# Local attention: probabilities divided before their transposition, attended rows straight out of PE in feature-major form

## The chip, the core and the metric

One core of one Trainium2 chip runs the whole program: a stack of four blocks over 8192 tokens of 128 features in float32. The metric is the device time of one execution in microseconds. The engines are PE (matrix products), DVE, ACT and POOL (elementwise work and reductions) and SP (transfers); each runs its own instruction list in order and waits on semaphores for the others. PE writes to eight banks (PSUM), 128 partitions x 512 float32 each, named `banks` in the rows; POOL cannot read them.

## The reference

The function touched is the local attention of the last block, in both of its layers (DEPTH = 2). The part that matters:

```python
q, k = l2norm(q) * q_scale, l2norm(k) * k_scale      # then rotary embedding
bk, bv = look_around(bk), look_around(bv)             # own window of 64 and the one before
sim = jnp.einsum('bhwid,bhwjd->bhwij', bq, bk)
sim = jnp.where(mask, -jnp.finfo(sim.dtype).max, sim)
attn = jax.nn.softmax(sim, axis=-1)
out = jnp.einsum('bhwij,bhwjd->bhwid', attn, bv)
# heads joined, out @ wo, added to the layer's input
```

Eight heads of 64 features, windows of 64 queries that see 128 keys. The softmax is exp(sim - row maximum) divided by the row's sum. Dividing commutes with the product with v, so it can be done before or behind it.

## The kernel before, in words

`local_attention` works in slots of one tile of 128 tokens; there are 64 slots in each layer, four in one round of a hardware loop (`rounds_of`). Slot k is software-pipelined over several tiles: it projects q and k of tile k+3, norms and rotates tile k+2, turns q and k of tile k+1, computes scores and exponentials of tile k, and multiplies tile k-1 with v. The order of work on each engine is what its own `slot(i, k)` writes down; nothing reorders it. Tiles with even k (L1852 in the scores) see the start of a sequence half, those with odd k (L1856) use `v_mixed`, which POOL puts together from two tiles' v.

One tile's path behind the scores, with names as in the rows:

- DVE reduces the raw scores (minus_raw, L2096) and scales the result (minus_max, L2100, from minus_raw and rnorm).
- ACT takes the exponentials of four heads (`exps(i, k, 0)`), later of the other four, with row sums (L2015). POOL's second cross product (L1925) also waits for minus_max.
- In the next slot PE transposes the probabilities of four heads (`pe_turn`, L1865), DVE copies them to SBUF (probs_t, L2080), PE multiplies with v (`pe_mix`, L1879) into bank 5, token-major; then the same for the other four heads.
- In the slot after that DVE takes the reciprocal of the row sums (L2085) and multiplies bank 5 by it (attended_tok, L2089); PE transposes the result in four pieces (L1995), ACT copies them to `ot` (L2060).
- One slot later still PE multiplies `ot` with the output weights (L1976) and DVE adds to xn (L2108).

Beside this DVE does the sums of squares (L2114), the straight part of the rotation (L2124, twice) and the sum with the crossed part (L2133, called the rotated sum below). POOL does the norm of k (L1935, `unit`), the crossed part of the rotation (L1925, twice), and, in turns, the shifted copy of tokens (L345, L346; even slots, once PE's v projection is through) or `v_mixed` (L1953, L1954; odd slots).

Banks 6 and 7 are shared in turn by the entries of MISC: the n-th use waits until the use two before it has been read.

## Time and profile before

| | us |
|---|---|
| median of 3 runs | 3130.24 (3124.16 to 3334.51) |
| profiled execution | 3113.36 |
| its span in the trace | 3111.6 |

| engine | busy us (share) | granted clock |
|---|---|---|
| PE | 2867.9 (92%) | 0.962 over the span |
| DVE | 2120.9 (68%) | |
| ACT | 2077.8 (67%) | |
| POOL | 1022.5 (33%) | |

The shares are means over all stages. Local attention is the stretch from about 1521 to 2140 us and that from about 2315 to 2940 us; between them and behind them stand the feed-forward parts. The ends of PE's instructions are modelled, and DVE's and POOL's instructions are recorded from the time they begin, held or not: an instruction that takes longer than its equals was held inside.

### The profile page before, as it was taken

The numbers are of one execution on the slowest core, as the hardware profiler recorded it, in microseconds if no ns is written. First come the engines' busy times: TensorE is split into PE (matmuls) and PEld (weight loads), VectorE is DVE, ScalarE is ACT, GpSimd is POOL, SyncE is SP. The second block draws the span as 40 slices with busy tenths as digits, with TensorE's granted clock in tenths as the row PEclk, the third lists the DMA queues.
The fourth block names the chain that finished last, engine by engine and source line by source line (L and its number), as shares of the span: only waits on it lengthen the run. The fifth ranks groups of instructions, "written<-read, shape, count | busy, mean of one in ns | idle before, by whom it ended". The sixth has DMA issues, their size and how long they took to land. (4 is left out here: it accounts for less than half of the span.)

```text
span 3111.6 us, 64366 instructions
## 1 busy us (share of the span) xinstructions
PE 2867.9 (92%) x19916; PEld 1800.0 (58%) x19916; DVE 2120.9 (68%) x3260; ACT 2077.8 (67%) x5545; POOL 1022.5 (33%) x1164
## 2 busy tenths in 40 slices
PE   6899999997999799778799999998989999999899
PEld 3577896763744234435466666665435666666543
DVE  4666555666844689657688878885437878888656
ACT  4466565667733744263388888886858888888686
POOL 0233343330000033110255555552225555555321
PEclk9899998999999999889899999998999999999999
DMA  4200220000000000220000000000000000000000
GB/s 137 75 20 21 59 66 18 20 17 12 1 15 1 0 1 1 55 31 0 26 2 0 0 0 0 0 0 19 1 8 2 0 0 0 0 0 0 1 21 34
DMA packets 82988, 51.48 MB, mean 17 GB/s; under 512 B 28848, under 2 KB 75568, under 8 KB 82864
## 3 DMA queue, kind: packets, MB, share of 16 engines
q1 hardware_dynamic: 78768, 41.56, 4.8%
q0 software_dynamic: 4096, 8.40, 0.9%
q8 instruction: 62, 1.02, 0.1%
q14 instruction: 62, 0.51, 0.1%
HBM read 31.59 MB, written 18.35 MB: 16 GB/s over the span
## 5 line engine op out<-in xcount | busy, mean ns | idle before, releaser
L1887 PE MATMUL banks<-weights,hf 128*128 128x512 f32 x768 | 436.8, 652 | 23.9 <-POOL hf L346 11.3
L2015 ACT ACTIVATE probs<-banks,minus_max,rnorm 128x128 f32<-128x128 f32 x1024 | 455.2, 465 | 3.1 <-DVE minus_max L2100 3.1
L1925 POOL TENSOR_TENSOR qk_cross<-qk_raw,rope_scaled 128x512 f32<-128x512 f32 x256 | 326.2, 1275 | 50.8 <-DVE minus_max L2100 33.3
L2080 DVE COPY probs_t<-banks 128x512 f32<-128x512 f32 x256 | 175.9, 687 | 134.6 <-PE banks L1865 134.0
L2015 ACT ACTIVATION_READ_ACCUMULATOR probs<-banks,minus_max,rnorm 128x1 f32 x1024 | 217.9, 213 | 0.0
L1935 POOL TENSOR_TENSOR qk_rot<-qk_rot,rnorm 128x512 f32<-128x512 f32 x128 | 133.6, 1044 | 256.4 <-DVE qk_rot L2133 244.0
L718 ACT ACTIVATE probs<-banks,minus_max 128x128 f32<-128x128 f32 (+1 forms) x512 | 208.3, 426 | 14.0 <-DVE minus_max L757 12.0
L2096 DVE TENSOR_REDUCE minus_raw<-banks 128x8 f32<-128x1024 f32 x128 | 156.8, 1225 | 55.5 <-PE banks L1852 32.4
L1879 PE MATMUL banks<-v_tok,probs_t 128*64 128x64 f32 x3072 | 174.6, 228 | 8.8 <-DVE probs_t L2080 3.8
L1879 PEld LDWEIGHTS banks<-v_tok,probs_t 128*64 128x64 f32 x3072 | 139.2, 137 | 71.4 <-issue 42.5
L2114 DVE TENSOR_REDUCE sumsq<-qk_sq 128x16 f32<-128x1024 f32 x128 | 154.8, 1209 | 27.0 <-issue 19.9
L2124 DVE TENSOR_TENSOR qk_rot<-qk_raw,rope_scaled 128x512 f32<-128x512 f32 x256 | 165.9, 689 | 5.8
L1896 PE MATMUL banks<-ident,qk_rot 128*128 128x128 f32 x1024 | 162.8, 282 | 4.7 <-DVE qk_rot L2133 4.7
L1887 PEld LDWEIGHTS banks<-weights,hf 128*128 128x128 f32 x768 | 117.2, 192 | 79.1 <-ACT kt L2041 21.2
L1865 PE MATMUL banks<-ident,probs 128*128 128x128 f32 x1024 | 160.8, 280 | 0.0
L2133 DVE TENSOR_TENSOR qk_rot<-qk_rot,qk_cross 128x1024 f32<-128x1024 f32 x128 | 159.2, 1244 | 0.2
L1865 PEld LDWEIGHTS banks<-ident,probs 128*128 128x128 f32 x1024 | 117.4, 141 | 71.9 <-issue 63.3
L756 DVE TENSOR_REDUCE minus_max<-banks 128x2 f32<-128x256 f32 x128 | 54.3, 424 | 124.8 <-PE banks L590 124.8
L1976 PE MATMUL banks<-ot,weights 128*128 128x128 f32 x1024 | 136.0, 276 | 1.6 <-ACT ot L2060 1.6
L345 POOL COPY hf<-xn 64x256 f32 (+1 forms) x64 | 57.8, 903 | 236.8 <-PE banks L1887 236.5
L2029 ACT ACTIVATE qk_sq<-qk_raw 128x1024 f32<-128x1024 f32 x128 | 134.3, 1049 | 0.1
L1896 PEld LDWEIGHTS banks<-ident,qk_rot 128*128 128x128 f32 x1024 | 114.9, 142 | 29.5 <-issue 21.0
(343 smaller groups left out, 7126.4 us busy)
## 6 DMA issues: line engine op xcount, KB each, us to landing
sorted_x<-zero_rows SPq DMA_DIRECT2D x10, 512.0 KB, 6.3
rows_in<-sorted_x SPq DMA_DIRECT2D x18, 256.0 KB, 3.1
sorted_y<-rows_out SPq DMA_DIRECT2D x18, 256.0 KB, 2.4
x_res<-in_x SPq DMA_DIRECT2D x8, 512.0 KB, 6.6
out_x<-x_res SPq DMA_DIRECT2D x16, 256.0 KB, 2.0
w1b<-in_L_ffn_w SPq DMA_DIRECT2D x8, 256.0 KB, 4.5
s_branch<-in_L_ffn_w SPq DMA_DIRECT2D x8, 256.0 KB, 6.5
w1g<-in_L_ffn_W SPq DMA_DIRECT2D x8, 256.0 KB, 3.0
```

The lines of the kernel that those rows point to most:

```text
L718: last = act.activation(pr[:, j % 2, e, span], ps[:, 2 * s + e, span], ACT.Exp, bias=nm[:, s, qb, e:e + 1], accum_out=sums[:, u, qb, head: ...
L1865: mm = pe.transpose(ps[:, 4, n * P:(n + 1) * P], pr[:, k % 2, 4 * h + n], m["ident"][:])
L1879: mm = pe.matmul(ps[64 * w:64 * w + 64, 5, at], pt[:, h, n * P + 64 * w:n * P + 64 * w + 64], vm[:, at] if tb and not w else va[:, k % 4, ...
L1887: pe.matmul(ps[:, misc(k, j)], hf[:, n // 2 % 2, 0, n % 2 * P:(n % 2 + 1) * P], wqkv[:, w:w + QW], start=True, stop=True).then_inc(*S[name ...
L1896: mm = pe.transpose(ps[:, misc(k, j), c * P:(c + 1) * P], st[:, n % 4, first:first + P], m["ident"][:])
L1925: return pool.tensor_tensor(by_half(tw[:, n, at]), by_half(qk[:, n, at])[:, :, ::-1, :], tab[:, n, 2 * w + 1].rearrange("p (a d) -> p a d" ...
L2015: last = act.activation(pr[:, k % 2, head], ps[:, 2 * (k % 2) + par, c * P:(c + 1) * P], ACT.Exp, scale=rn[:, k % 4, head:head + 1], bias= ...
L2080: dve.tensor_copy(pt[:, h], ps[:, 4]).then_inc(*S["turned_sb"].inc)
L2096: dve.tensor_reduce(nr[:].rearrange("p (b c) -> p b c", b=2), ps[:, 2 * (k % 2):2 * (k % 2) + 2].rearrange("p b (c t) -> p b c t", c=4), A ...
L2114: dve.tensor_reduce(ss[:], by_head(sq[:]), AX.X, ALU.add).then_inc(*S["sumsq"].inc)
L2124: last = dve.tensor_tensor(by_head(st[:, n, at]), by_head(qk[:, n % 2, at]), tab[:, n % 2, 2 * w:2 * w + 1].to_broadcast([P, HEADS, DH]), ...
L2133: dve.tensor_tensor(st[:, n], st[:, n], tw[:, n % 2], ALU.add).then_inc(*S["rotated"].inc)
```

## The change

The reciprocal and the division move in front of the transposition. For heads 4 to 7 DVE multiplies the probabilities of tile k-1 (`half`), for heads 0 to 3 POOL does (`weigh`), in one product of 128x512 each. `pe_mix` now takes v as the weights and probs_t as what streams, so that a head's rows come out of PE with the features on the partitions; ACT copies bank 5 to `ot`, and L1995, L2089 and bank uses of the transposed result go. The output projection and the addition to xn come one slot earlier, and at another place in the slot.

```diff
-MISC = [("qt_sb", 1), ("added", -3), ("q_sb", 3), ("kt_sb", 1), ("k_sb", 3), ("v_sb", 1), ("ot_sb", -2)]
+MISC = [("qt_sb", 1), ("q_sb", 3), ("kt_sb", 1), ("k_sb", 3), ("v_sb", 1), ("added", -2)]
...
         def pe_turn(pe, i, k, h):
-            pe.wait_ge(*S["exps"].at(i, 2 * k + h))
+            pe.wait_ge(*S["masked" if h else "weighed"].at(i, k))
...
+            width = P // (1 + tb)
             for n in range(4):
-                at = slice((4 * h + n) * DH, (4 * h + n + 1) * DH)
-                for w in range(2):
-                    mm = pe.matmul(ps[64 * w:64 * w + 64, 5, at], pt[:, h, n * P + 64 * w:n * P + 64 * w + 64],
-                                   vm[:, at] if tb and not w else va[:, k % 4, at], start=True, stop=True)
+                head = 4 * h + n
+                at = slice(head * DH, (head + 1) * DH)
+                rows = slice(head % 2 * 64, head % 2 * 64 + 64)
+                for w in range(1 + tb):
+                    first = head // 2 * P + w * width
+                    mm = pe.matmul(ps[rows, 5, first:first + width],
+                                   vm[:, at] if tb and not w else va[:, k % 4, at],
+                                   pt[:, h, n * P + w * width:n * P + (w + 1) * width], start=True, stop=True)
...
+                def weigh(i, k):
+                    pool.wait_ge(*S["rowsum"].at(i, 2 * k))
+                    pool.tensor_tensor(pr[:, k % 2, 0:4], pr[:, k % 2, 0:4],
+                                       rs[:, k % 2, 0:4].unsqueeze(2).to_broadcast([P, 4, P]), ALU.mult)\
+                        .then_inc(*S["weighed"].inc)
...
                         pool.wait_ge(*S["copied"].at(i, k // 2 + 2))
+                    if here(i, k):
+                        weigh(i, k)
...
                     if here(i, k - 2):
-                        pe_free(pe, i, k, OT_AT)
-                        pe.wait_ge(*S["attended"].at(i, k - 2))
+                        pe_free(pe, i, k, OUT_AT)
+                        pe.wait_ge(*S["ot_sb"].at(i, k - 2))
                         for c in range(4):
-                            mm = pe.transpose(ps[:, misc(k, OT_AT), c * P:(c + 1) * P], o[:, c * P:(c + 1) * P],
-                                              m["ident"][:])
-                        mm.then_inc(*S["ot_ps"].inc)
+                            mm = pe.matmul(ps[:, misc(k, OUT_AT), 0:P], wo[:, c], ot[:, c], start=(c == 0), stop=(c == 3))
+                        mm.then_inc(*S["o_ps"].inc)
...
                 def slot(i, k):
+                    if here(i, k - 2):
+                        act.wait_ge(*S["mixed"].at(i, 2 * (k - 2) + 1))
+                        act.wait_ge(*S["o_ps"].at(i, k - 3))
+                        act.activation(ot[:], bank(ps, 5, 4, P), ACT.Copy).then_inc(*S["ot_sb"].inc)
...
+                def inverse(i, k, h):
+                    heads = slice(4 * h, 4 * h + 4)
+                    dve.wait_ge(*S["exps"].at(i, 2 * k + h))
+                    if h == 0:
+                        dve.wait_ge(*S["weighed"].at(i, k - 2))
+                    dve.reciprocal(rs[:, k % 2, heads], sums[:, k % 2, heads]).then_inc(*S["rowsum"].inc)
...
+                    if here(i, k - 1):
+                        inverse(i, k - 1, 1)
+                        dve.wait_ge(*S["rowsum"].at(i, 2 * (k - 1) + 1))
+                        half = pr[:, (k - 1) % 2, 4:]
+                        dve.tensor_tensor(half, half, rs[:, (k - 1) % 2, 4:].unsqueeze(2).to_broadcast([P, 4, P]), ALU.mult)\
+                            .then_inc(*S["masked"].inc)
                     if here(i, k - 1):
                         turned(i, k - 1, 0)
```

On DVE, a slot in the middle of the loop, before and then now (L2080 and L2089 COPY are the same copies; line numbers moved by nine or more):

```order
L2096 TENSOR_REDUCE minus_raw<-banks 128x8 [waits rowmax,rnorm,scores]
L2100 TENSOR_TENSOR minus_max<-minus_raw,rnorm 128x8 [waits rawmax]
...
L2108 TENSOR_TENSOR xn<-xn,banks 128x128
...
L2080 COPY probs_t<-banks 128x512 [waits mixed]
...
L2080 COPY probs_t<-banks 128x512 [waits mixed,turned]
L2133 TENSOR_TENSOR qk_rot<-qk_rot,qk_cross 128x1024 [waits crossed,straight]
...
L2085 RECIPROCAL inv_sums<-row_sums 128x8 [waits exps]
...
L2089 TENSOR_TENSOR attended_tok<-banks,inv_sums 128x512 [waits ot_ps,mixed]
```

```order
L2103 TENSOR_REDUCE minus_raw<-banks 128x8 [waits rowmax,rnorm,scores]
L2107 TENSOR_TENSOR minus_max<-minus_raw,rnorm 128x8 [waits rawmax]
...
L2096 RECIPROCAL inv_sums<-row_sums 128x4 [waits exps]
...
L2115 TENSOR_TENSOR probs<-probs,inv_sums 128x512 [waits rowsum]
...
L2089 COPY probs_t<-banks 128x512 [waits mixed]
...
L2096 RECIPROCAL inv_sums<-row_sums 128x4 [waits weighed]
...
L2089 COPY probs_t<-banks 128x512 [waits mixed]
L2143 TENSOR_TENSOR qk_rot<-qk_rot,qk_cross 128x1024 [waits crossed,straight]
...
L2148 TENSOR_TENSOR xn<-xn,banks 128x128
```

A reciprocal and a product of the probabilities now stand between minus_max and the first turned copy, a second reciprocal in front of the second copy; the addition to xn went from the slot's front to its end.

On POOL, an even slot's end and the next slot's start in the loop now; before, the same rows without L1937:

```order
L1930 TENSOR_TENSOR qk_cross<-qk_raw,rope_scaled 128x512 [waits rowmax]
...
L345 COPY hf<-xn 64x256
...
L346 COPY hf<-xn 64x255
...
L1937 TENSOR_TENSOR probs<-probs,inv_sums 128x512 [waits rowsum]
L1946 TENSOR_TENSOR qk_rot<-qk_rot,rnorm 128x512 [waits rotated,rnorm]
...
L1930 TENSOR_TENSOR qk_cross<-qk_raw,rope_scaled 128x512 [waits rotated,k_sb,q_sb]
```

POOL's product stands last in its slot, in front of the norm of the next tile's k and its two cross products.

On PE, from the value projection to the q transposes of the next slot, before and now:

```order
L1887 MATMUL banks<-weights,hf 128x512
L1995 MATMUL banks<-ident,attended_tok 128x128 x4
...
L1879 MATMUL banks<-v_tok,probs_t 64x64 x8
L1845 MATMUL banks<-hide,ident_bf 128x512 x2
L1852 MATMUL banks<-kt,qt 128x128 x8
...
L1896 MATMUL banks<-ident,qk_rot 128x128 x4
...
L1976 MATMUL banks<-ot,weights 128x128 x4
```

```order
L1892 MATMUL banks<-weights,hf 128x512
L2006 MATMUL banks<-ot,weights 128x128 x4
...
L1883 MATMUL banks<-probs_t,v_tok 64x128 x4
...
L1845 MATMUL banks<-hide,ident_bf 128x512 x2
L1852 MATMUL banks<-kt,qt 128x128 x8
...
L1901 MATMUL banks<-ident,qk_rot 128x128 x4
...
L1892 MATMUL banks<-weights,hf 128x512
```

The output projection took the place of the four transposes, and the q projection follows the q transposes directly. In the rows of the trace every float32 product is two instructions (two passes), a transposition one.

## Rows read from the trace of the kernel before

**Rows 1.** Busy time of the engines in one stretch: us, busy (xinstructions), PEclk, DMA share, GB/s.
```profile
1700.00:1800.00 100.00, 99.19 (x993) 66.52 (x993) 81.15 (x129) 85.56 (x265) 55.29 (x55) 1.00 0.00 0
```
**Rows 2.** Row-maximum reduction in 1600 to 2050: xcount, ns min/median/max, first and last start.
```profile
L2096 DVE TENSOR_REDUCE minus_raw<-banks x48: 1223/1225/1226, 1600.5 to 2042.2; 128x8 f32<-128x1024 f32 x48
```
**Rows 3.** Instructions of DVE in order: start us, us, what, idle before.
```profile
1732.13 1.23 DVE L2096 TENSOR_REDUCE minus_raw<-banks 128x8 f32<-128x1024 f32 x1 [0.57 <-PE banks L1852]
1733.39 0.17 DVE L2100 TENSOR_TENSOR minus_max<-minus_raw,rnorm 128x8 f32<-128x8 f32 x1
1733.68 0.29 DVE L2108 TENSOR_TENSOR xn<-xn,banks 128x128 f32 x1
1735.02 0.69 DVE L2080 COPY probs_t<-banks 128x512 f32<-128x512 f32 x1 [1.05 <-PE banks L1865]
...
1738.33 0.68 DVE L2080 COPY probs_t<-banks 128x512 f32<-128x512 f32 x1
1738.93 1.21 DVE L2133 TENSOR_TENSOR qk_rot<-qk_rot,qk_cross 128x1024 f32<-128x1024 f32 x1
1740.07 0.19 DVE L2085 RECIPROCAL inv_sums<-row_sums 128x8 f32<-128x8 f32 x1
1740.45 0.69 DVE L2089 TENSOR_TENSOR attended_tok<-banks,inv_sums 128x512 f32<-128x512 f32 x1 [0.19 <-DVE inv_sums L2085]
1741.59 1.22 DVE L2096 TENSOR_REDUCE minus_raw<-banks 128x8 f32<-128x1024 f32 x1 [0.45 <-PE banks L1856]
...
1744.40 0.69 DVE L2080 COPY probs_t<-banks 128x512 f32<-128x512 f32 x1 [0.97 <-PE banks L1865]
```
**Rows 4.** Instructions of PE in the same stretch.
```profile
1737.62 1.12 PE L1887 MATMUL banks<-weights,hf 128*128 128x512 f32 x2
1738.58 0.60 PE L1995 MATMUL banks<-ident,attended_tok 128*128 128x128 f32 x4
1739.72 0.60 PE L1845 MATMUL banks<-hide,ident_bf 128*128 128x512 bf16 x2
...
1741.79 1.06 PE L1976 MATMUL banks<-ot,weights 128*128 128x128 f32 x8
1742.71 1.12 PE L1887 MATMUL banks<-weights,hf 128*128 128x512 f32 x2
```
**Rows 5.** Instructions of POOL in the same stretch.
```profile
1733.64 1.27 POOL L1925 TENSOR_TENSOR qk_cross<-qk_raw,rope_scaled 128x512 f32<-128x512 f32 x1 [0.68 <-DVE minus_max L2100]
1738.94 1.46 POOL L345 COPY hf<-xn 64x256 f32 x1 [4.03 <-PE banks L1887]
1740.44 0.40 POOL L346 COPY hf<-xn 64x255 f32 x1
1740.92 1.04 POOL L1935 TENSOR_TENSOR qk_rot<-qk_rot,rnorm 128x512 f32<-128x512 f32 x1
```
**Rows 6.** DVE and POOL meeting: two instructions in order, and three lines in 1600 to 2050.
```profile
1555.39 0.63 DVE L2100 TENSOR_TENSOR minus_max<-minus_raw,rnorm 128x8 f32<-128x8 f32 x1
...
1554.73 2.64 POOL L1925 TENSOR_TENSOR qk_cross<-qk_raw,rope_scaled 128x512 f32<-128x512 f32 x2
...
L2100 DVE TENSOR_TENSOR minus_max<-minus_raw,rnorm x48: 166/214/371, 1601.8 to 2043.5; 128x8 f32<-128x8 f32 x48
L1925 POOL TENSOR_TENSOR qk_cross<-qk_raw,rope_scaled x96: 1265/1274/1286, 1600.4 to 2043.9; 128x512 f32<-128x512 f32 x96
L345 POOL COPY hf<-xn x24: 391/924/1461, 1607.1 to 2039.6; 64x256 f32 x24
```
**Rows 7.** PE during the first mix of an odd tile, in order.
```profile
1736.35 0.27 PE L1879 MATMUL banks<-v_mixed,probs_t 128*64 128x64 f32 x1
...
1736.46 0.22 PE L1879 MATMUL banks<-v_mixed,probs_t 128*64 128x64 f32 x1
1736.46 0.22 PE L1879 MATMUL banks<-v_tok,probs_t 128*64 128x64 f32 x1
1736.52 0.22 PE L1879 MATMUL banks<-v_mixed,probs_t 128*64 128x64 f32 x1
...
1736.97 0.44 PE L1865 MATMUL banks<-ident,probs 128*128 128x128 f32 x2
```

More of the change, by code:

```diff
@@ L1780, in conv_mixer @@
         S["loaded"].base += 16 * len(ahead)
-MISC = [("qt_sb", 1), ("added", -3), ("q_sb", 3), ("kt_sb", 1), ("k_sb", 3), ("v_sb", 1), ("ot_sb", -2)]
-QT_AT, OUT_AT, Q_AT, KT_AT, K_AT, V_AT, OT_AT = range(7)
+MISC = [("qt_sb", 1), ("q_sb", 3), ("kt_sb", 1), ("k_sb", 3), ("v_sb", 1), ("added", -2)]
+QT_AT, Q_AT, KT_AT, K_AT, V_AT, OUT_AT = range(6)
 def local_weights(area, a, layer):
@@ L1813, in local_attention @@
         nr, nm = buf("minus_raw", P, HEADS), buf("minus_max", P, 2, HEADS)
-        sums, rs = buf("row_sums", P, 2, HEADS), buf("inv_sums", P, HEADS)
-        o, ot = buf("attended_tok", P, QW), buf("ot", P, 4, P)
+        sums, rs = buf("row_sums", P, 2, HEADS), buf("inv_sums", P, 2, HEADS)
+        ot = buf("ot", P, 4, P)
         def here(i, n, per=4):
@@ L1871, in pe_mix @@
             if h == 0:
-                pe.wait_ge(*S["attended"].at(i, k - 1))
+                pe.wait_ge(*S["ot_sb"].at(i, k - 1))
                 pe.wait_ge(*S["v_sb"].at(i, k))
@@ L1900, in local_attention @@
                              "rnorm", "crossed", "rotated", "unit", "qt_ps", "kt_ps", "qt_sb", "kt_sb", "scores",
-                             "rawmax", "rowmax", "rowsum", "attended", "ot_ps", "ot_sb", "o_ps", "added"], 4)
-        per.update(copied=2, v_mixed=2, g2=2, exps=8, turned=8, turned_sb=8, mixed=8)
+                             "rawmax", "rowmax", "ot_sb", "o_ps", "added"], 4)
+        per.update(copied=2, v_mixed=2, g2=2, exps=8, rowsum=8, weighed=4, masked=4, turned=8, turned_sb=8, mixed=8)
         with Stage(R, **per), nc.Block() as block:
@@ L1951, in slot @@
                             pool.wait_ge(*S["crossed"].at(i, k + 2))
+                        if here(i, k - 1):
+                            pool.wait_ge(*S["weighed"].at(i, k - 1))
                         pool.sem_inc(S["g2"].sem, 1)
@@ L1971, in slot @@
                         pe_turn_qk(pe, i, k, QT_AT, "qt")
-                    if here(i, k - 3):
-                        pe_free(pe, i, k, OUT_AT)
-                        pe.wait_ge(*S["ot_sb"].at(i, k - 3))
-                        for c in range(4):
-                            mm = pe.matmul(ps[:, misc(k, OUT_AT), 0:P], wo[:, c], ot[:, c], start=(c == 0), stop=(c == 3))
-                        mm.then_inc(*S["o_ps"].inc)
                     if here(i, k + 3):
@@ L2009, in exps @@
                     act.wait_ge(*S["turned"].at(i, 2 * (k - 2) + h))
[L2010 to L2011 removed]
+                    act.wait_ge(*S["rowsum"].at(i, 2 * (k - 2) + h))
                     for n in range(4):
@@ L2056, in slot @@
                         act.activation(va[:, (k + 1) % 4], ps[:, misc(k, V_AT)], ACT.Copy).then_inc(*S["v_sb"].inc)
-                    if here(i, k - 2):
-                        act.wait_ge(*S["ot_ps"].at(i, k - 2))
-                        act.wait_ge(*S["o_ps"].at(i, k - 3))
-                        act.activation(ot[:], bank(ps, misc(k, OT_AT), 4, P), ACT.Copy).then_inc(*S["ot_sb"].inc)
                     if here(i, k):
@@ L2103, in slot @@
                             .then_inc(*S["rowmax"].inc)
-                    if here(i, k - 3):
-                        xn = m["xn"][:, bass.ds((i * 4 + k - 3) * P, P)]
-                        dve.wait_ge(*S["o_ps"].at(i, k - 3))
-                        dve.wait_ge(S["first"].sem, PRIME)
-                        dve.tensor_tensor(xn, xn, ps[:, misc(k, OUT_AT), 0:P], ALU.add).then_inc(*S["added"].inc)
+                    if here(i, k - 1):
+                        inverse(i, k - 1, 1)
[3 more added lines that the diff above has]
+                            .then_inc(*S["masked"].inc)
                     if here(i, k - 1):
@@ L2126, in slot @@
                         last.then_inc(*S["straight"].inc)
+                    if here(i, k):
+                        inverse(i, k, 0)
                     if here(i, k - 1):
@@ L2133, in slot @@
                         dve.tensor_tensor(st[:, n], st[:, n], tw[:, n % 2], ALU.add).then_inc(*S["rotated"].inc)
+                    if here(i, k - 2):
+                        xn = m["xn"][:, bass.ds((i * 4 + k - 2) * P, P)]
+                        dve.wait_ge(*S["o_ps"].at(i, k - 2))
+                        dve.wait_ge(S["first"].sem, PRIME)
+                        dve.tensor_tensor(xn, xn, ps[:, misc(k, OUT_AT), 0:P], ALU.add).then_inc(*S["added"].inc)
                 rounds_of(dve, R, 1, 1, lambda i: [slot(i, k) for k in range(4)])
```

13 lines of the change are left out of this document (2 added, 11 removed).

## The prediction, made before the changed kernel was timed

> **What bounds the kernel now.** The diff touches one function, `local_attention`, which runs once for each of the two layers; so I first read busy time by stage, then the engines' rows over two neighbouring slots. In a stretch in the middle of the first layer [rows 1] the granted clock is 1.00 (the 2.4 GHz level) and PE is recorded as busy 99%, ACT 86%, DVE 81%, POOL 55%. PE's ends are modelled, so the 99% alone does not make PE the bound. The pace is the distance between two starts of the row-maximum reduction, one per slot: 48 of them from 1600.5 to 2042.2 us [rows 2], so 441.7 / 47 = 9.40 us. There are 64 slots in each of two layers, 128 x 9.40 = 1203 us of the 3113.4 us of the profiled execution.
>
> What paces a slot is read from DVE and PE together. Let R be the start of the reduction in the even slot, 1732.13 [rows 3]. The first turned copy (probs_t) starts at R+2.89, released by PE's transposes after an idle 1.05. The second turned copy starts at 1738.33, 3.31 later, with DVE busy all the way between them. PE's second mix needs that copy; the next mask matmul (L1845), which is queued right behind the mix, starts at 1739.72 [rows 4], 1.39 later; and the scores behind it let the next reduction start at 1741.59, 1.87 later. 2.89 + 3.31 + 3.26 = 9.46. So a slot is a loop: DVE work, mix, scores, DVE work. The only slack in it on DVE is the 0.97 to 1.05 in front of the first turned copy, and there PE is what is late: between scores and the transposes of the probabilities it does the q transposes, the output projection L1976 (0.92 to L1887, 1741.79 to 1742.71) and the q projection [rows 4].
>
> **The change, part by part.**
>
> *PE.* The four transposes L1995 go (0.60), and the output projection moves from its place in front of the q projection into theirs. They stood while PE was going to wait for the second turned copy anyway, so taking them out gives nothing by itself. Moving the projection brings the transposes of the probabilities 0.92 forward, to about R+1.9. In its new place it follows the value projection; behind the end of the first turned copy PE has a mix (0.62, 1736.35 to 1736.97 [rows 7]), transposes 0.60, value projection 0.96 (1737.62 to 1738.58 [rows 4]) and output projection 0.92 = 3.1 us, against 3.4 us that DVE takes from that end to the end of the second copy. Hidden, with 0.3 to spare.
>
> *The mixes.* In even slots eight 64x64 products become four of 64x128, alternating between the two column halves: the same time. In odd slots the two windows of one head now come one after the other in the same half. Before, neighbours in different halves start together, a pair every 0.06 us (1736.46, 1736.52 [rows 7]). If starts must keep the order of the program, the second window of a head waits 0.11 for the first (two passes), but the next head's first can run beside it, so a mix grows by one such step, 0.11. Bounds: 0, if the halves run freely, and 0.44 if nothing overlaps at all. I take 0.05 of the second mix in every odd slot, 62 x 0.05 = 3 us; the first mix has PE slack. The Trainium skill (TensorE: Matmul & The Clock Gate, Part 3, packing small matmuls) says that matmuls keep program order in start and end; by that the term would be 7 us, and without it 0.
>
> *ACT.* The copy to `ot` changes place and source, no work is added. The second half's exponentials start earlier by the length of that copy. ACT is idle in 14% of a slot, 1.3 us, and nothing in the loop above waits for it. Nothing.
>
> *DVE, without regard to POOL.* The product behind the mix goes (0.69, with its wait for the reciprocal 0.38 from start to start [rows 3]); it stood where DVE waited for scores, so this gives nothing. In the loop two things are added. Between the row maximum and the first turned copy: a reciprocal in the place of the addition to xn (R+1.55, as 1733.68), 0.38 later the product of four heads, R+1.93, and with 0.69 for it (the row of attended_tok, the same 128x512) and the usual start 0.08 before the predecessor's end, the first turned copy at R+2.54. That is 0.35 earlier than now. Between the two copies: a second reciprocal, 0.12 to 0.19, so 3.43 for 3.31. A slot would be 2.54 + 3.43 + 3.26 = 9.23.
>
> *POOL, and what it does to DVE.* POOL gets one more product (128x512, as L1935, 1.04 [rows 5]); with 55% of 9.4 busy, 5.2 us, it has the time. But the new DVE product reads two tensors in SBUF, and it comes just when POOL works. The second of POOL's two cross products waits for the row maximum: it starts at 1733.64 [rows 5], R+1.51, 0.08 after DVE's minus_max ends, and takes 1.27 [rows 6], to R+2.78. What happens when two such meet is in the trace. The tiny minus_max (128x8) takes 0.17 when POOL is idle and 0.63 at 1555.39, where it ends at 1556.02; POOL's first cross product ran from 1554.73 to 1556.00 [rows 6]. In the stretch its times run from 166 to 371 ns. The other way round, POOL's copy L345 takes 391 ns or 1461: the long one starts at 1738.94 beside DVE's rotated sum, which runs from 1738.93 to 1740.14, and ends 0.26 behind it [rows 3, 5]. So a DVE product of two SBUF tensors and a reading POOL instruction do not overlap: who is first finishes. DVE's addition to xn and its copies from the banks are not held. The Trainium skill (SBUF — State Buffer, SBUF: two separate sides) states this as an exclusive lock on a shared pair of ports, taken for the whole instruction by whoever starts first, for DVE instructions with two SBUF inputs against POOL instructions that read SBUF. By that rule the sum is slower than before, without it the 9.23 above holds; the trace agrees with it.
>
> The new product is ready at R+1.93, POOL began at R+1.51: it is held until POOL is through. minus_max ended 0.02 after POOL with 0.17 of its own, so it effectively began 0.15 before POOL's end; the product then ends at 2.78 - 0.15 + 0.69 = 3.32, and the turned copy starts at 3.24. Even slot: 3.24 + 3.43 + 3.26 = 9.93.
>
> In the odd slot POOL is later. At the end of the even one it has its two copies, the new product and `unit` (1.04) to do. The rotated sum starts at R+3.24+3.43+0.60 = 7.27 and ends at 8.48; POOL's product, queued behind the copies at about 7.4, is held to 8.4 and ends at 9.4; unit ends at 10.45, the first cross product at 11.77. The next reduction is at 9.93, so minus_max, held as before, ends at 1.86 instead of 1.43, and all behind it is 0.43 later: 10.36. Behind the odd slot (no shift copies, so POOL's product comes first, from 7.25 to 8.3, and holds the rotated sum to an end of 9.36, which is not in the loop) unit begins at 9.5 and the cross product ends at 11.8, 1.45 behind the next reduction: minus_max ends at 1.47 for 1.43, which I leave out. A pair of slots: 20.29 against 18.80, +1.49. I count 31 pairs per layer (the first and last slots are not in the steady order): 62 x 1.49 = +92 us.
>
> *The end of each layer.* Reciprocal, product and transposes (0.19 + 0.69 + 0.60) leave the drain: -3 us in two layers.
>
> **Sum:** 92 + 3 - 3 = +92 us on 3113.4, so 3205. The runs shown have a median of 3130.2, 17 us above the profiled execution; I take half of that and predict **3213 us**, 2.7% over the median. For one measurement 2%, 63 us, is about what can be told from no change.
>
> **The rivals.**
>
> 1. *The product comes first* (0.18). If reciprocal and product get in before POOL's cross product begins to read, POOL waits and DVE does not: 9.23 a slot, 124 x -0.17 = -21 us, some 3092 to 3109 us: not slower. For it: only 0.4 us lie between them. Against: POOL needs one semaphore after minus_max (0.08), DVE a whole reciprocal and its completion. It decides at 1.51 against 1.93. The same time comes out if the hold does not apply to a product with a repeated operand.
> 2. *POOL falls behind in every slot* (0.10). Then minus_max is held in even slots too, and shift copies that slip between two DVE products cost 0.4 in every other slot: 124 x 0.96 + 25 = +144, 3257 to 3274 us. It needs unit to begin later than 0.9 before the next reduction; even slots are past that by 0.4 and odd ones just on it, so a little more delay on POOL decides. Against: in odd slots POOL's product has no DVE product in front of it.
> 3. *Others* (0.08): PE's longer waits (0.4 to 1.3 us a slot) let the granted clock fall to its 1.2 GHz level in part of the stage, far slower (0.01); the holds hit but are half as long, within 2% (0.03); DVE's path is shorter than I think and more than 2% is gained, for which no row speaks (0.04).
>
> Forecast: 0.64, and of this 0.08 lies under 2% (if the odd slot is not delayed: 124 x 0.53 = 66, less the drain: 3176 to 3193). Slower: 0.56 + 0.10 + 0.01 = 0.67. Same: 0.08 + 0.18 + 0.03 = 0.29. Faster: 0.04. The range is 3100 to 3268: it takes in the forecast with both bounds, most of rival 2 and the upper part of rival 1. The forecast's own range is 3176 to 3240.
>
> **What would show it.** Right: the new DVE product of the probabilities recorded at about 1.4 us instead of 0.69, ending with POOL's second cross product; minus_max at about 0.6 in every other slot; reductions 10.1 us apart; PE idle more, its mix still released by the turned copy; ACT with 2 us of idle time. Wrong: the product at 0.7 and the cross product recorded as longer than 1.27 (rival 1); a pace under 9.4; the second mix released by the output projection instead of DVE; the new odd mix longer than 0.8 us.

## The result, and the profile after

The changed kernel takes 3202.8 us (median of 4 runs, 3201.7 to 3205.6) against 3131.2 us beside it: ratio 1.0239, 95% interval [1.0226, 1.0252]. It is slower by 2.4%. The forecast was 3213 us, the range 3100 to 3268, and "slower by over 2%" had 0.67. Ratios leave out two executions of the kernel before in a slow state of the chip, 3334.5 us and one of 7150.0 us beside e5 to e8.

The first view is the same stretch as in [rows 1], then the line of the row-maximum reduction as in [rows 2], with the lines that meet on DVE and POOL below it (count, ns min/median/max, first and last start).

```profile
1700.00:1800.00 100.00, 87.35 (x797) 56.66 (x798) 89.23 (x131) 79.86 (x250) 59.81 (x60) 1.00 0.00 0
```
```profile
L2103 DVE TENSOR_REDUCE minus_raw<-banks x45: 1223/1224/1226, 1602.1 to 2044.4; 128x8 f32<-128x1024 f32 x45
L2107 DVE TENSOR_TENSOR minus_max<-minus_raw,rnorm x45: 166/541/616, 1603.4 to 2045.7; 128x8 f32<-128x8 f32 x45
L2115 DVE TENSOR_TENSOR probs<-probs,inv_sums x45: 1733/1771/1779, 1604.1 to 2046.3; 128x512 f32<-128x512 f32 x45
L1937 POOL TENSOR_TENSOR probs<-probs,inv_sums x45: 1039/1799/1814, 1599.9 to 2042.1; 128x512 f32<-128x512 f32 x45
L1930 POOL TENSOR_TENSOR qk_cross<-qk_raw,rope_scaled x90: 1265/1271/1282, 1602.6 to 2046.3; 128x512 f32<-128x512 f32 x90
```

PE fell from 99% busy to 87%, DVE rose from 81% to 89%, at the same granted clock of 1.00 (2.4 GHz). The pace is 442.3 / 44 = 10.05 us a slot, against 9.40. Every one of the 45 products on DVE took 1.73 to 1.78 us, though its equal took 0.69 in [rows 3]; POOL's cross products kept their 1.27 [rows 6]. So where these two meet, DVE pays and POOL does not.

Two slots of DVE after (start, duration, what, idle before), to be laid beside [rows 3], and POOL beside [rows 5]:

```profile
1732.83 1.22 DVE L2103 TENSOR_REDUCE minus_raw<-banks 128x8 f32<-128x1024 f32 x1 [0.57 <-PE banks L1852]
1734.08 0.41 DVE L2107 TENSOR_TENSOR minus_max<-minus_raw,rnorm 128x8 f32<-128x8 f32 x1
1734.42 0.17 DVE L2096 RECIPROCAL inv_sums<-row_sums 128x4 f32<-128x4 f32 x1
1734.62 1.77 DVE L2115 TENSOR_TENSOR probs<-probs,inv_sums 128x512 f32<-128x512 f32 x1
1736.32 0.68 DVE L2089 COPY probs_t<-banks 128x512 f32<-128x512 f32 x1
...
1739.65 0.66 DVE L2089 COPY probs_t<-banks 128x512 f32<-128x512 f32 x1
1740.23 1.22 DVE L2143 TENSOR_TENSOR qk_rot<-qk_rot,qk_cross 128x1024 f32<-128x1024 f32 x1
...
1742.73 1.22 DVE L2103 TENSOR_REDUCE minus_raw<-banks 128x8 f32<-128x1024 f32 x1 [1.10 <-PE banks L1856]
1743.99 0.61 DVE L2107 TENSOR_TENSOR minus_max<-minus_raw,rnorm 128x8 f32<-128x8 f32 x1
```
```profile
1733.20 2.64 POOL L1930 TENSOR_TENSOR qk_cross<-qk_raw,rope_scaled 128x512 f32<-128x512 f32 x2
...
1740.53 1.81 POOL L1937 TENSOR_TENSOR probs<-probs,inv_sums 128x512 f32<-128x512 f32 x1 [0.16 <-POOL hf L346]
1742.30 1.04 POOL L1946 TENSOR_TENSOR qk_rot<-qk_rot,rnorm 128x512 f32<-128x512 f32 x1
1743.31 2.64 POOL L1930 TENSOR_TENSOR qk_cross<-qk_raw,rope_scaled 128x512 f32<-128x512 f32 x2
```

POOL's second cross product ends at 1733.20 + 2.64 = 1735.84, DVE's product at 1736.39: 0.55 apart, the product's own 0.69 less 0.14. The reverse case is at 1740.23: DVE's rotated sum runs to 1741.45 and POOL's product, 1.04 by itself, is recorded as 1.81.

DVE's copies, its sums of squares and its addition to xn are as short as before.

What PE waited for in 1600 to 2050 (us in total, times, longest), with 44 slots in the stretch. The same view of the kernel before has no line at all: PE waited for nobody.

```profile
PE banks L1883 <- DVE probs_t L2089: 37.8, 78, 0.8
PE banks L1892 <- ACT qk_raw L2048: 18.2, 45, 0.5
```

The whole span grew by 88.9 us (3111.6 to 3200.5). Within the layers, from the first to the last of 64 reductions, it is 43.0 + 44.1 = 87.1; another 8.1 lies ahead of the first reduction (1546.2, now 1554.3), and the stretch between the layers is 6.1 shorter. The 8.1 is not a cost of the loop: in the kernels of this study that first reduction falls anywhere from 1538.9 to 1563.9, although nothing ahead of the function differs. It goes with the group of runs and not with the edit: 1538.9 to 1544.9 in e1 to e4, 1559.6 to 1563.9 in e5 to e8, 1555.7 to 1559.6 in e9 and e10, and each group ran on a chip of its own. All that lies outside the two layers does the same: 1928.4 to 1929.6 us in e1 to e4, 1949.8 to 1952.9 in e5 to e8, 1944.0 and 1944.3 in e9 and e10, 1939.8 in the change, 1938.0 before. What differs between the groups is not known. For this reason the table below also gives the length of the two layers added up, which this scatter doesn't touch.

That column has a weakness of its own. It is one trace for each kernel, and the traced execution of the kernel before, 3113.4 us, is 17.8 us below the median of the runs beside the change, while that of the change lies on its median. By medians the change costs 71.7 us, by the traces 88.9. In which stage the other executions of the kernel before spend the 17 us is not shown. So the column carries comparisons between the changed kernels; against the kernel before, differences under some 18 us need the ratio as well.

| kernel | median us | ratio to before | slot us | two layers us |
|---|---|---|---|---|
| before | 3131.2 | 1 | 9.40 | 1173.6 |
| the change | 3202.8 | 1.0239 [1.0226, 1.0252] | 10.05 | 1260.7 |
| e1_fills | 3088.1 | 0.9922 [0.9891, 0.9953] | 9.23 | 1157.1 |
| e2_no_product | 3087.4 | 0.9920 [0.9888, 0.9951] | 9.24 | 1156.4 |
| e3_swap | 3128.0 | 1.0052 [1.0038, 1.0067] | 9.62 | 1201.1 |
| e4_cross_late | 3141.6 | 1.0090 [1.0064, 1.0117] | 9.69 | 1212.5 |
| e5_banks | 3127.3 | 0.9998 [0.9977, 1.0018] | 9.40 | 1175.3 |
| e6_moved | 3172.2 | 1.0132 [1.0111, 1.0154] | 9.77 | 1220.4 |
| e7_free | 3161.0 | 1.0102 [1.0083, 1.0122] | 9.64 | 1207.8 |
| e8_qfirst | 3215.9 | 1.0278 [1.0255, 1.0301] | 10.07 | 1261.0 |
| e9_late | 3119.7 | 0.9967 [0.9953, 0.9981] | 9.35 | 1170.8 |
| e10_late_mix | 3114.7 | 0.9949 [0.9933, 0.9966] | 9.32 | 1166.4 |

(e1 to e4 ran beside a median of 3111.1 us of the kernel before, e5 to e8 beside 3130.8, e9 and e10 beside 3130.7. e1 and e2 leave out a part of the work: e1 the crossed part of the rotation, e2 the division of heads 4 to 7.)

### The profile page after: what moved, and what is told of

Its sections match the earlier page's. It is cut to its first block and busy times, and to the rows that moved or that the text cites. A ratio compares the mean times of both kernels' runs of the same rounds, so it can differ in the third digit from the quotient of the medians.

```text
span 3200.5 us, 61524 instructions
## 1 busy us (share of the span) xinstructions
PE 2812.7 (88%) x18380; PEld 1737.6 (54%) x18380; DVE 2293.6 (72%) x3388; ACT 2077.6 (65%) x5545; POOL 1151.0 (36%) x1292
## 5 line engine op out<-in xcount | busy, mean ns | idle before, releaser
L1892 PE MATMUL banks<-weights,hf 128*128 128x512 f32 x768 | 417.7, 627 | 67.8 <-ACT qk_raw L2048 52.8
L1937 POOL TENSOR_TENSOR probs<-probs,inv_sums 128x512 f32<-128x512 f32 x128 | 177.8, 1389 | 176.3 <-DVE inv_sums L2096 166.6
L1883 PE MATMUL banks<-probs_t,v_tok 128*64 128x128 f32 (+1 forms) x2048 | 158.3, 255 | 73.8 <-DVE probs_t L2089 73.5
L2115 DVE TENSOR_TENSOR probs<-probs,inv_sums 128x512 f32<-128x512 f32 x128 | 219.1, 1712 | 4.4
L2143 DVE TENSOR_TENSOR qk_rot<-qk_rot,qk_cross 128x1024 f32<-128x1024 f32 x128 | 190.6, 1489 | 0.1
L1883 PEld LDWEIGHTS banks<-probs_t,v_tok 128*64 128x64 f32 x2048 | 113.6, 138 | 137.8 <-DVE probs_t L2089 137.1
L2089 DVE COPY probs_t<-banks 128x512 f32<-128x512 f32 x256 | 171.2, 669 | 6.4 <-PE banks L1865 6.3
L2037 ACT ACTIVATE qt<-banks 128x512 f32<-128x512 f32 x128 | 76.5, 598 | 150.5 <-PE banks L1901 150.5
L2006 PEld LDWEIGHTS banks<-ot,weights 128*128 128x128 f32 x1024 | 135.9, 194 | 61.1 <-issue 61.1
L1946 POOL TENSOR_TENSOR qk_rot<-qk_rot,rnorm 128x512 f32<-128x512 f32 x128 | 133.3, 1042 | 87.1 <-DVE qk_rot L2143 83.9
L2006 PE MATMUL banks<-ot,weights 128*128 128x128 f32 x1024 | 136.8, 277 | 1.6 <-ACT ot L2033 1.6
```

The lines of the kernel that those rows point to most:

```text
L1883: mm = pe.matmul(ps[rows, 5, first:first + width], vm[:, at] if tb and not w else va[:, k % 4, at], pt[:, h, n * P + w * width:n * P + (w ...
L1892: pe.matmul(ps[:, misc(k, j)], hf[:, n // 2 % 2, 0, n % 2 * P:(n % 2 + 1) * P], wqkv[:, w:w + QW], start=True, stop=True).then_inc(*S[name ...
L1937: pool.tensor_tensor(pr[:, k % 2, 0:4], pr[:, k % 2, 0:4], rs[:, k % 2, 0:4].unsqueeze(2).to_broadcast([P, 4, P]), ALU.mult)\
L2006: mm = pe.matmul(ps[:, misc(k, OUT_AT), 0:P], wo[:, c], ot[:, c], start=(c == 0), stop=(c == 3))
L2089: dve.tensor_copy(pt[:, h], ps[:, 4]).then_inc(*S["turned_sb"].inc)
L2115: dve.tensor_tensor(half, half, rs[:, (k - 1) % 2, 4:].unsqueeze(2).to_broadcast([P, 4, P]), ALU.mult)\
```

## The experiments

The theory: DVE's product and POOL's second cross product both read two tensors in SBUF and don't overlap, and DVE is second. The rivals: the product is slow by itself, or any work of POOL slows it, or the loss is PE's new order. First both sides of the meeting are taken away, then its timing is changed, then the operand.

**e1_fills: POOL writes instead of reading.**

```diff
-                        cross(i, k, 0)
+                        fill(i, k, 0)
...
+                def fill(i, k, w):
+                    pool.memset(tw[:, (k + 2) % 2, w * QW:(w + 1) * QW], 0.0)
+                    return pool.memset(spare[:, (k + 2) % 2, w, :], 0.0)
```

> POOL's two cross products of a slot are replaced by fills that write the same place and a spare buffer in about the same time (0.53 + 0.67 us each) but read nothing; the crossed part of the rotation is left out of the result. Theory (a DVE product of two SBUF tensors waits for a POOL instruction that reads SBUF): DVE's product of the probabilities falls from 1.77 to about 0.69 us and minus_max to 0.17, the pace from 10.05 to about 8.8 us a slot, the total to about 3045 us. Rival 1 (any work of POOL, also mere writing, slows DVE): product and pace stay, about 3200 us. Rival 2 (the product is slow by itself, from its in-place or repeated operand): product stays at 1.77, about 3200 us.

```profile
1738.77 0.17 DVE L2112 TENSOR_TENSOR minus_max<-minus_raw,rnorm 128x8 f32<-128x8 f32 x1
1738.86 0.18 DVE L2101 RECIPROCAL inv_sums<-row_sums 128x4 f32<-128x4 f32 x1
1739.08 0.69 DVE L2120 TENSOR_TENSOR probs<-probs,inv_sums 128x512 f32<-128x512 f32 x1
```
```profile
1738.84 0.64 POOL L1938 MEMSET spare<- 128x660 f32 x1
1739.43 0.52 POOL L1937 MEMSET qk_cross<- 128x512 f32 x1
1739.90 0.64 POOL L1938 MEMSET spare<- 128x660 f32 x1
```

DVE's product takes 0.69 while POOL is writing the whole time, and in all 49 slots of the stretch it takes 691 to 693 ns. So a busy POOL isn't enough: it must read. The whole loss is gone and more, 87.1 us turn into -16.5. The pace expected was 8.8 and came out 9.23. PE's waits say why: DVE never holds it up now, and it waits 19.8 us in 49 places, all for ACT's copy of the queries. The floor is PE's.

```profile
PE banks L1892 <- ACT qk_raw L2053: 19.8, 49, 0.5
```

**e2_no_product: the other side taken away.**

```diff
-                        dve.tensor_tensor(half, half, rs[:, (k - 1) % 2, 4:].unsqueeze(2).to_broadcast([P, 4, P]), ALU.mult)\
-                            .then_inc(*S["masked"].inc)
+                        dve.reciprocal(spare[:], sums[:, (k - 1) % 2, 4:]).then_inc(*S["masked"].inc)
```

> DVE's product of the probabilities is replaced by a second tiny reciprocal with the same semaphores; the division of heads 4 to 7 is left out. It prices the product in its place. Theory (product plus hold lie on the path): the pace falls by 1.3 to 1.6 us a slot until PE's own work of some 8.4 us is near, total 3005 to 3045 us. Rival (only the product's own 0.69 us counts, the hold falls into time that is waited anyway): about 3115 us. Rival (the loop is set by PE): under 20 us gained.

The layers have the same length as in e1 within 0.7 us, 1156.4. The pace fell by 0.81 us to 9.24, not by the expected 1.3 to 1.6, since PE's floor lies there and not at 8.4. POOL's products stand, minus_max is still held (166 to 772 ns), and it costs nothing, since DVE has time before PE needs it. So the product's 1.77 is what carries the loss. Whether its own 0.69 would matter this run can't tell; e1 has it and is as fast.

**e3_swap: the turned copy first.**

```diff
+                        turned(i, k - 1, 0)
+                    if here(i, k - 1):
                         inverse(i, k - 1, 1)
...
-                    if here(i, k - 1):
-                        turned(i, k - 1, 0)
```

> On DVE the first turned copy goes in front of the reciprocal and product of heads 4 to 7; nothing else changes. Theory (the loss is the place: the product arrives while POOL's second cross product reads): copy and mix no longer wait for it and it arrives 0.9 us later, so it is held 0.2 to 0.5 us instead of 1.1; about 9.3 us in even and 9.65 us in odd slots, total 3110 to 3145 us, about the kernel before. Rival (the product costs its queue time wherever it stands before the second copy): 3180 to 3205 us.

The product comes later and meets less of the cross product: 727/981/1179 ns for 1771. Of the 87.1 us 59.6 come back; the median, 3128.0, lies in the expected 3110 to 3145. What is left is the rest of the hold and minus_max, up to 961 ns, and PE still waits for probs_t, 12.4 us in 23 places. A reordering lessens such a hold and doesn't end it.

**e4_cross_late: POOL waits for DVE's product.**

```diff
                         cross(i, k, 0)
-                        if here(i, k):
-                            pool.wait_ge(*S["rowmax"].at(i, k))
+                        if here(i, k - 1):
+                            pool.wait_ge(*S["masked"].at(i, k - 1))
```

> POOL's second cross product waits for DVE's product of the probabilities instead of for minus_max. Theory: the product is held only by what is left of the first cross product, it takes 0.7 to 1.1 us instead of 1.77; the hold comes back in part at the rotation's straight products in odd slots (v_mixed copies later); 9.3 to 9.55 us a slot, total 3107 to 3139 us. Rival (POOL's whole chain sets the pace, so that a later cross product only delays it): 3200 us or more.

```profile
1742.80 0.93 DVE L2107 TENSOR_TENSOR minus_max<-minus_raw,rnorm 128x8 f32<-128x8 f32 x1
1743.65 0.17 DVE L2096 RECIPROCAL inv_sums<-row_sums 128x4 f32<-128x4 f32 x1
1743.85 0.69 DVE L2115 TENSOR_TENSOR probs<-probs,inv_sums 128x512 f32<-128x512 f32 x1
```
```profile
1742.43 1.27 POOL L1930 TENSOR_TENSOR qk_cross<-qk_raw,rope_scaled 128x512 f32<-128x512 f32 x1
1744.62 1.28 POOL L1930 TENSOR_TENSOR qk_cross<-qk_raw,rope_scaled 128x512 f32<-128x512 f32 x1 [0.92 <-DVE probs L2115]
```

The product is 0.69 in all 46 slots: the same instruction as in the change, the same operands, only not beside a reading POOL. That a product of two SBUF tensors with a repeated operand is slow by itself is excluded. The product is also still written in its own place, so that is excluded too. But the holds come back elsewhere: the other cross product now holds minus_max (to 1743.73; up to 980 ns in the stretch), the straight products of the rotation take up to 1096 ns for 688, and PE waits for probs_t 17.1 us in 23 places. The slot is 9.69, over the 9.3 to 9.55 that was expected. 48.2 of the 87.1 us come back.

**e5_banks: one operand from the banks.** ACT writes the exponentials of heads 4 to 7 back into their score banks; DVE's product reads them there.

```diff
-                        last = act.activation(pr[:, k % 2, head], ps[:, 2 * (k % 2) + par, c * P:(c + 1) * P], ACT.Exp,
+                        score = ps[:, 2 * (k % 2) + par, c * P:(c + 1) * P]
+                        last = act.activation(score if h else pr[:, k % 2, head], score, ACT.Exp,
...
-            pe.wait_ge(*S["exps"].at(i, 2 * (k - 2) + 1))
+            pe.wait_ge(*S["masked"].at(i, k - 2))
```

> ACT writes the exponentials of heads 4 to 7 back into the score banks, and DVE's product reads them there, so that it has one operand in SBUF (the reciprocals) instead of two; work, order and size are the same, POOL is as it was. Theory (only an instruction with two SBUF operands is held by a reading POOL): the product takes 0.69 us and is not held, minus_max still is (0.2 to 0.6); the pace is 9.3 to 9.45 us, or PE's floor of 9.22 where the other two kernels without the hold stood; ratio to the kernel before 0.990 to 1.003, about 3100 to 3140 us on the first chip. Rival (any DVE instruction beside POOL's products is slowed, or it is the repeated operand that is slow): product at 1.4 to 1.8 us, ratio about 1.024.

```profile
1746.64 0.17 DVE L2108 TENSOR_TENSOR minus_max<-minus_raw,rnorm 128x8 f32<-128x8 f32 x1
1746.75 0.18 DVE L2097 RECIPROCAL inv_sums<-row_sums 128x4 f32<-128x4 f32 x1
1746.96 0.69 DVE L2116 TENSOR_TENSOR probs<-banks,inv_sums 128x512 f32<-128x512 f32 x1
```
```profile
1745.49 2.67 POOL L1930 TENSOR_TENSOR qk_cross<-qk_raw,rope_scaled 128x512 f32<-128x512 f32 x2
```

This is the run that decides. POOL's cross products run from 1745.49 to 1748.16, the DVE product lies wholly inside, from 1746.96 to 1747.65, and takes 0.69. It takes 690 to 692 ns in all 48 slots. Same size, same engine, same time, same neighbour; what differs is the place of one operand, and with it that the product no longer overwrites what it reads, which e4 has cleared. The small minus_max, still with two operands in SBUF, is held as before or longer (166/615/987), which is the other half of the comparison in the same trace. The layers shrink by 85.4 us to 1175.3, 1.7 more than before. The Trainium skill (SBUF — State Buffer, SBUF: two separate sides) says that a DVE operation "with two SBUF inputs" takes the shared port as an exclusive lock only against a POOL operation that reads SBUF. By that rule the product runs free in e1 and e5 and is held in the change; the traces agree on all three.

**e6_moved: the kernel before with only the output projection (and the addition to xn) moved.** Both stand at the places that they have in the change (L2006, L2148), but still serve tile k-3; the four transposes L1995 and the product behind the mix stay.

> The kernel before with one part of the change alone: the output projection (and the addition to xn) moved behind the value projection, in front of the transposes of the attended rows, which stay. Theory (DVE has about 1 us of slack in front of the first copy, then PE's own work is the floor, some 9.2 us with the four transposes): 9.2 to 9.3 us a slot for 9.40, ratio 0.991 to 0.997. Rival (moving it is the whole use of the change, DVE's loop of 8.5 us shows): ratio 0.965 to 0.97. Rival (PE then reaches the second mix later than the second copy): ratio 1.00 to 1.02.

The layers grow by 46.8 us, and not through DVE: minus_max is 166 to 169 ns, DVE is 77% busy, and PE never waits for it. (One operation of DVE is held, the scaling of the sums of squares, 174/312/611 ns, without a wait of PE behind it.) PE is never without work except in this wait, 46 times in 1600 to 2050:

```profile
PE banks L1887 <- ACT qk_raw L2035: 18.6, 46, 0.5
```

So the move by itself costs. Take the wait away, 0.40 a slot, and PE's own work is 9.77 - 0.40 = 9.37 us; before the change a slot was 9.40. PE was full. With the transposes gone and the mix in its new form (e1) the same sum is 9.23 - 0.41 = 8.82: these were worth 0.55 us a slot, and the new wait for ACT takes 0.41 of it. The subtraction is rough: in the other kernels without the transposes it gives 8.63 (e8) to 8.93 (e3, e5), always below the two with them. The expectation, a gain of 0.3 to 0.9%, failed. Of its rivals the one with PE late at the second mix (1.00 to 1.02) gave the time: 1.0132, and PE waits for no turned copy at all.

**e7_free: four things at once.** As e5_banks; both cross products behind the row maximum; ACT's copy of the queries in front of its squares; neighbours of the odd mix in different column groups.

> The kernel with the product out of the banks, and three steps more: both cross products of POOL wait for minus_max (so that minus_max is not held), ACT copies q in front of the squares (so that PE's k projection, which waits 0.4 us for that copy where the hold is gone, does not), and the odd mixes alternate between the column halves. Theory: no hold on the loop but 0.3 us at the straight products of odd slots; DVE loop 8.75 to 9.05 us, PE 8.8; pace 8.8 to 9.1 us, ratio 0.975 to 0.988, faster than both kernels. Rival (the shared read path of DVE and POOL is used 9 us a slot and is the bound wherever the pieces stand): pace 9.2 or more, ratio 0.993 or more.

```profile
1739.16 0.65 PE L1865 MATMUL banks<-ident,probs 128*128 128x128 f32 x4
1740.68 1.12 PE L1892 MATMUL banks<-weights,hf 128*128 128x512 f32 x2 [0.86 <-ACT kt L2055]
1741.64 1.05 PE L2006 MATMUL banks<-ot,weights 128*128 128x128 f32 x8
```

minus_max and the product are not held any more (166/166/170 and 690/691/692), and yet a slot is 9.64. The straight products are (up to 1095 ns) and the rotated sum is (up to 1704), but PE does not wait for DVE once in the stretch. The wait for the query copy is gone; in its place PE's value projection waits 0.86 for ACT's kt copy, 42.0 us in 47 slots, because the bank is the one that the copy must empty and ACT reaches it later. A wait of 0.41 was exchanged for one of 0.89. The expected 8.8 to 9.1 failed. The rival, 9.2 or more because the shared read path is the bound, gave the number but not the cause: the wait is for ACT, and e9 and e10, with the same work on that path, take 0.3 us a slot less.

**e8_qfirst: the change with only ACT's copy in front of its squares.**

> The changed kernel with one edit: ACT copies q in front of the squares. Theory (in the changed kernel DVE's held product sets the pace and PE's wait for the q copy costs nothing): no difference to the changed kernel, ratio to before 1.020 to 1.026. Rival (PE's wait of 0.39 us for the copy is on the loop): 0.3 us a slot less, ratio 1.011 to 1.014.

The two layers take 1261.0 us against 1260.7, the slot 10.07. PE's wait for ACT is gone and its waits for probs_t grew from 37.8 to 63.0 us: it arrives earlier and waits longer for DVE. In the change DVE sets the pace, so what PE gains is worth nothing; the control holds. The ratio, 1.0278, is 0.4% above that of the change. It comes from outside the two layers, 1952.9 us for 1939.8, where e5 to e7 with 1949.8 to 1951.5 lie as well; why is open.

**e9_late: e7 without its reordering of ACT and of the mix.** The only edit to e5_banks:

```diff
-                        cross(i, k, 0)
                         if here(i, k):
                             pool.wait_ge(*S["rowmax"].at(i, k))
+                        cross(i, k, 0)
```

> The changed kernel with the exponentials of heads 4 to 7 written back into their score banks (as e5_banks), and both of POOL's cross products behind the row maximum, so that the negation (minus_max) is held by neither. Theory (VectorE operations with two operands in SBUF and POOL's share a read path): minus_max 0.17 us and the product 0.69 us in every slot; the loop of VectorE then falls below TensorE's own work, and the pace is TensorE's, 9.2 to 9.3 us a slot (9.40 in e5_banks), or 3,110 to 3,125 us in all. The cross products start 0.4 us later, so the rotated sum moves with them, which nobody waits for as long as POOL is idle between them. Rival (the order of the cross product matters to the next queries and keys: ScalarE's copy of the queries waits for the crossed product, and TensorE's k projection for that copy): the wait of TensorE on that copy grows from 0.4 us by the 0.4 us of the delay, and the pace is 9.6 us as in e7_free, 3,160 us.

**e10_late_mix: e9 with the odd mix in another order.**

```diff
-            for n in range(4):
-                head = 4 * h + n
...
-                for w in range(1 + tb):
+            for pair in range(2):
+                for w, n in itertools.product(range(1 + tb), (2 * pair, 2 * pair + 1)):
+                    head = 4 * h + n
```

> e9_late, and the matmuls of odd slots' mixing ordered so that neighbours write to different column groups. Theory: the start cost of same-column neighbours (0.08 us on the odd mix, every second slot) goes, so at most 0.04 us a slot, 2 to 3 us in all below e9_late. Rival: the pace is not set by TensorE there, and nothing changes.

Of e9, the line of its negation (minus_max) and that of its product; of the change and then of e10, start and end of the odd mix:

```profile
L2108 DVE TENSOR_TENSOR minus_max<-minus_raw,rnorm x48: 166/167/170, 1605.6 to 2045.2; 128x8 f32<-128x8 f32 x48
L2116 DVE TENSOR_TENSOR probs<-banks,inv_sums x48: 690/691/692, 1605.9 to 2045.5; 128x512 f32<-128x512 f32 x48
```
```profile
1740.36 0.34 PE L1883 MATMUL banks<-probs_t,v_mixed 128*64 128x64 f32 x4 [0.17 <-DVE probs_t L2089]
...
1741.03 0.61 PE L1845 MATMUL banks<-hide,ident_bf 128*128 128x512 bf16 x2
```
```profile
1746.80 0.34 PE L1883 MATMUL banks<-probs_t,v_mixed 128*64 128x64 f32 x4
...
1747.42 0.61 PE L1845 MATMUL banks<-hide,ident_bf 128*128 128x512 bf16 x2
```

e9 is the first version with all of the work that is ahead of both kernels, 0.9967 [0.9953, 0.9981], by 0.3%; e10 gives 0.9949 [0.9933, 0.9966], and its layers are 4.4 us shorter than e9's. From the mix's start to the mask matmul it is 0.62 us in e10 and, in the change, 1731.08 - 1730.49 = 0.59 in an even slot and 0.67 in an odd one. So neighbours in the same column group (the same 64 of PE's 128 columns) cost an odd mix 0.05 us (0.67 to 0.62), or 0.08 against an even one. With 64 odd tiles in the two layers and two mixes in each that would be 128 x 0.05 = 6.4 us, of which 4.4 were seen, in one trace each. The 2 to 3 us expected were reckoned too low; why two of the six are missing was not followed.

e9's expectation of 9.2 to 9.3 was missed by 0.05: PE waits for probs_t in 12 of the 47 slots, 4.9 us, beside 19.4 us for ACT's query copy. That the latter is 0.41 a slot as in e5 excludes the rival. It also clears the late cross products of e7's loss; with the mix cleared by e10, e7's 9.64 is left to ACT's order, its only other edit, by elimination and by PE's wait for the kt copy.

## Why the prediction was right

It named the operation, the partner, the size and the effect on the pace. By its steps:

- **The hold** was its decisive term, argued from meetings in the trace of before [rows 6]. DVE's product ends 0.55 us behind POOL's cross product, forecast 0.54. The recorded length is 1.77, not "about 1.4": it starts 0.14 earlier (R+1.79 for R+1.93, since it follows the reciprocal at 0.20 and not 0.38) and ends 0.24 later, as POOL's cross product ends 0.23 later. e1, e4 and e5 show the mechanism from three sides: no read by POOL, no meeting in time, no second SBUF operand.
- **The even slot**: first turned copy at R+3.49 for 3.24, copy to copy 3.33 for 3.43, to the next reduction 3.08 for 3.26; sum 9.90 for 9.93. The total is better than its parts, which is luck: one came out 0.25 too low, the others 0.28 too high together. The second cross product ends at R+3.01 and not R+2.78, because POOL has fallen back in this slot as well: its first cross product still runs when minus_max is ready (0.41 for 0.17), and the second follows without a gap, where before it had waited 0.68 for DVE [rows 5]. In every second even slot minus_max is free (0.17 at 1754.33). On the other side, the reduction at 1742.73 starts 0.07 us behind the recorded end of the scores (1742.66), where it was 0.23; why is open.
- **The odd slot**: R+3.69 for 3.67, and behind it POOL's product holds DVE's rotated sum to R+9.31, forecast 9.36. The slot itself was forecast as 10.36 and is 10.34, but only every second time; the odd slots between are 10.06, which was not foreseen and whose cause was not followed. Mean pace 10.05 for the 10.14 that a pair of 20.29 gives.
- **The sum**: the loss in a slot was 0.65 us for the 0.745 forecast, 81 us for the 92 in the 124 steady slots. The layers still grew by 87.1, since the slots at their ends, put at nothing, lost some 5 us as well. The 3 us for the mixes were of the right size (an odd mix is 0.67 for the 0.62 of [rows 7]); the 3 us for the drain can't be told, since the stretch between the layers scatters from 200.4 to 205.4 us among the later kernels, against 206.5 before.
- **PE idles**, waiting for the turned copies 78 times, and ACT has 2.0 us idle a slot, both as told.
- **The half of the gap between profiled time and median**, +8 us: the profiled execution after, 3202.2, lies on its median. Here there was nothing to add, and 3205, the sum by itself, would have been 2 us off. That would have been luck: the sum starts from a traced execution 17.8 us below its median, and against the medians the loss is 71.7 us, not 92. The forecast of 3213 stands 83 us above the median it was made from; it is 10 us too high.

One step was wrong, though it didn't decide. "The 99% alone does not make PE the bound" was true as a sentence and wrong as a reading: the list of waits of before has no line for PE in 450 us, which means that PE itself was full. The loop through DVE was close behind: the second turned copy ended at 1739.01, and the mix began at 1739.11, when PE was through with its transposes. For this reason the four transposes did not stand in a wait, and "taking them out gives nothing by itself" fails. e6 puts a price on it: with the transposes kept, the moved projection costs 46.8 us; without them, and with the new mix, PE has about 0.55 us a slot to give. And the move was not free either. "Nothing" for ACT overlooked that PE's k projection comes earlier and now waits 0.41 us a slot for ACT's copy of the queries, which stands behind its squares. The two errors nearly cancel, by luck: the pace without a hold was forecast as 9.23 and is 9.23 in e1, for another reason, PE's work of 8.82 and that wait.

Rival 1 (POOL waits, not DVE) fell: all 45 products on DVE were long and none of the 90 cross products was over 1.28, so POOL was first each time. Its other form, no hold for a repeated operand, fell with the same rows, and e4 and e5 show that the length comes from the meeting and not from the operand. Its price, -21 us, was about right (-16.5 in e1). Rival 2 (POOL late in every slot) came half true: minus_max is held in every second even slot too, by 0.24, but the shift copies (L345) slipped between no two DVE products (391 ns in all 22), so the 0.4 it priced there didn't come. Of rival 3 nothing is seen: the granted clock stayed at 1.00 in the stretch, and the holds have their full length.

## What to carry to other kernels

Before moving elementwise work onto DVE, list what POOL reads at that moment: a DVE operation with two tensors in SBUF costs about its own time plus what is left of POOL's instruction, here 1.77 for 0.69. If it must stand there, give it an operand in a bank; that was worth 85 us here, more than swapping (60) or making POOL wait (48). And read the list of waits together with the busy share: an engine at 99% without any wait is full, and work taken from it is real time as soon as no other loop is as long.

## What the runs showed of the hardware

- A very small operation can be held too, even with one tensor. In e1 DVE's scaling of 128x16 takes 0.55 us for its 0.17 beside POOL's copy:

```profile
1741.53 0.55 DVE L2129 TENSOR_SCALAR sumsq<-sumsq 128x16 f32<-128x16 f32 x1
```
```profile
1741.43 0.61 POOL L1972 COPY v_mixed<-v_tok 64x512 f32<-64x512 f32 x1
```

  The same operation took up to 611 ns (median 312) in e6. The one before it in e1, a reduction of 128x1024 from SBUF, ran its usual 1.21 beside the copies. The Trainium skill (VectorE: DVE Perf Modes, Mode 2×_2P — use both read ports for one tensor) has it that a float32 operation with a constant in place of its second tensor may use both read ports; by that rule it is held as a product of two tensors is, and this row agrees.
- With a hold, the record contains the wait. POOL's instruction ends, and DVE's held one ends its own duration less about 0.15 later (0.55 behind for 0.69). In the other direction POOL's held copy ended 0.26 behind DVE [rows 3, 5].
- Between POOL's two cross products, back to back, DVE gets in: minus_max at 1734.08 was let through after the first (0.41), and the product behind it had to wait for the whole second.
- If the two take turns, the change has little room left, by an estimate from these rows: a slot has some 5.6 us of POOL's reading work (2.54 cross products, 1.04 each for the division and the norm, 1 for the copies) and 3.4 us of DVE's two-tensor work (0.17, 0.69, 1.3, 1.2), 9.0 of 10.05 us. Before it was 7.3 of 9.40. Each meeting overlaps by the 0.15 us above, so a reordering of the change could reach a little under 9 us at best; the two here that keep all of its work and the product in SBUF reached 9.62 (e3) and 9.69 (e4).
